# Two-layer cross-attention and expert kernel: hand-laced order of the first thirteen attention units, and a later rounding in steps 5, 9 and 13

## The reference

```python
ln_out = _ln(hidden_states, ln_w, ln_b)
q = _ln(_fp8_linear_pertensor(ln_out, wq, ...).reshape(b, s, g, hpg, d), qln_w, qln_b)
k = _ln(_fp8_linear_pertensor(ln_out, wk, ...).reshape(b, s, g, d), kln_w, kln_b)
v = _fp8_linear_pertensor(ln_out, wv, ...).reshape(b, s, g, d)
core = _gqa(q, k, v)            # self-attention, 16 query heads, 8 key heads
qx = _ln(_fp8_linear_pertensor(ln_out, wqx, ...))
kx, vx = split(cond @ w_kv_x)   # 64 context rows
xout = _gqa(qx, _ln(kx), vx)    # cross-attention, 16 query heads
catq = _div_clamp_fp8(concat([core, xout]), proj_smooth)
x = x + catq @ wproj * (proj_in_scale * proj_w_scale)
```

## Time and profile before

| | us |
|---|---|
| median of 3 runs | 832.49 (832.32 to 833.77) |
| the profiled execution | 832.6 |
| its span, first to last record | 830.8 |
| PE busy | 780.1 (94%) |
| DVE busy | 652.9 (79%) |
| ACT busy | 536.1 (65%) |
| POOL busy | 485.0 (58%) |

### The profile page before, as it was taken

One profiled execution on the slowest core, in us unless ns is written; L12 is line 12 of the kernel. 1 busy time (PEld: TensorE's weight loads), 2 busy tenths in 40 slices (PEclk: granted clock), 3 DMA queues, 4 the chain that ended last, 5 costly groups with the idle time before them and its releaser, 6 DMA issues.

```text
span 830.8 us, 14410 instructions
## 1 busy us (share of the span) xinstructions
PE 780.1 (94%) x4848; PEld 666.3 (80%) x4848; DVE 652.9 (79%) x1509; ACT 536.1 (65%) x1236; POOL 485.0 (58%) x858
## 2 busy tenths in 40 slices
PE   3588999999999999999999999999999999999997
PEld 2466788898788888888888878898888787777787
DVE  6878999899988999889889796676665658887644
ACT  6788887787877878778765465533332257986432
POOL 2588968859697696877876287425220124637510
PEclk9789999999999999999999999999999999999999
DMA  7000120011200112000200321986613000001001
GB/s 245 13 1 1 39 64 14 2 39 39 77 1 2 39 39 77 2 1 1 69 27 8 108 69 41 230 208 203 212 62 102 25 1 15 16 12 39 1 1 51
DMA packets 29224, 45.59 MB, mean 55 GB/s; under 512 B 4128, under 2 KB 18272, under 8 KB 29024
## 3 DMA queue, kind: packets, MB, share of 16 engines
q1 hardware_dynamic: 27760, 41.31, 16.8%
q10 hardware_dynamic: 1392, 3.37, 1.2%
HBM read 43.49 MB, written 1.18 MB: 54 GB/s over the span
## 4 chain that ended last, share of the span: by engine, by line
PE 64%; DVE 18%; ACT 9%; issue 4%; DMA 2%; SPq 1%; POOL 1%; ACTq 0%; DVEq 0%
PE PS L889 17%; PE PS L959 8%; PE PS L749 6%; PE PS L844 4%; PE PS L818 3%; PE PS L780 3%; PE PS L1073 3%; DVE st L1840 2%; PE PS L801 2%; PE PS L771 2%; PE PS L790 2%; PE PS L1025 2%; ACT P L1238 2%; DVE yb L1742 2%; PE PS L1035 1%
## 5 line engine op out<-in xcount | busy, mean ns | idle before, releaser
L2539 POOL TENSOR_SCALAR raw<-raw,mvq,rsq 128x128 f32<-128x128 f32 x312 | 183.7, 607 | 1.6
L889 PE MATMUL PS<-xq,WH 128*128 128x512 f32 x472 | 149.3, 398 | 0.0
L889 PEld LDWEIGHTS PS<-xq,WH 128*128 128x128 f32 x472 | 86.2, 189 | 17.5 <-issue 1.9
L749 PE MATMUL PS<-WH,xq 128*128 128x256 f32 (+1 forms) x256 | 88.5, 365 | 8.7 <-DVE xq L1746 6.2
L889 PE MATMUL PS<-xq,WL 128*128 128x512 f32 x236 | 92.7, 393 | 0.0
L749 PE MATMUL PS<-WL,xq 128*128 128x256 f32 (+1 forms) x256 | 84.7, 350 | 0.0
L1238 ACT ACTIVATE P<-PS,sm 128x256 f32<-128x256 f32 x128 | 61.1, 498 | 23.5 <-DVE sm L1904 23.4
L959 PE MATMUL PS<-xq,m_hh 128*128 128x256 f32 x384 | 70.2, 283 | 2.5 <-ACT m_hh L1124 1.3
L1840 DVE BATCH_NORM_STATS2 st<-raw 128x6 f32<-128x128 f32 x320 | 70.4, 276 | 1.7 <-ACT raw L1210 1.7
L818 PE MATMUL PS<-PT,vr 128*128 128x256 f32 x256 | 66.5, 382 | 3.8 <-ACT PT L1124 3.7
L780 PE MATMUL PS<-kT,qT 128*128 128x256 f32 x256 | 65.9, 380 | 1.9 <-ACT qT L1227 1.9
(11 more groups left out here) (316 smaller groups left out, 2154.7 us busy)
## 6 DMA issues: line engine op xcount, KB each, us to landing
wst<-in_wgu SPq DMA_DIRECT2D x24, 256.0 KB, 2.7
wst<-in_wall SPq DMA_DIRECT2D x18, 256.0 KB, 3.0
l_KM<-share SPq DMA_DIRECT2D x9, 384.0 KB, 3.7
dst<-in_wdn SPq DMA_DIRECT2D x24, 128.0 KB, 2.7
wst<-in_wkvx SPq DMA_DIRECT2D x8, 256.0 KB, 3.3
m_pre<-in_wo ACTq DMA_DIRECT2D x1, 2048.0 KB, 11.7
l_KM<-share SPq DMA_DIRECT2D x6, 256.0 KB, 6.6
l_S<-share SPq DMA_DIRECT2D x6, 256.0 KB, 6.2
```

What stands on the lines that cost most here:

```text
L749: t = e.matmul(PS[:, b, o:o + n], xq[s][:, k, c * 128:(c + 1) * 128], W[:, k, w0:w0 + n], start=(k == 0 and i == 0), stop=(k == 1 and i == 1))
L889: t = e.matmul(PS[:, b, :], W[wi][:, gu, k, :], a[:, k, cols], start=(n == 0), stop=(n == 5))
L2539: t = e.tensor_scalar(v, v, mvq[:, par, n, 0:1], rsq[:, par, n:n + 1], ALU.add, ALU.mult)
```

## The change

In all four lists the first thirteen units (n from 0 to 12, that is up to step 2, unit 2) are written out one call after another instead of coming from the loop, and the loops begin at BEGUN = 13. The calls are the same, in another order. On DVE the generators of quantise, stats, stats_x, begin_q, round_y and the layer norm are advanced one instruction at a time by go(generator, times); a, b and c are the stats of the three parts, q the quantisations, r the begin_q, y the roundings, lr the rest of the layer norm, xs stats_x. ln_root is rewritten so that its steps can be taken singly. On POOL norm_q is split into root_q (Newton) and norm_q(s, h) for one head, and the load_w of the next group's parts 4, 5 and 0 stand inside norm_q(2). DVE's semaphore for its own steps is no longer changed after the start. Apart from that, AHEAD loses (5, 4), (9, 4) and (13, 4): in these units DVE does the maxima first and then the rounding. The diff, cut:

```diff
@@ -18,6 +18,7 @@
 NEG = 1e30
 STEPS = 16
 PARTS = (2, 0, 1)
+BEGUN = 13
 P2ORDER = (4, 0, 1, 2, 3)
 QPAIRS = [(h, z) for h in range(4) for z in (1, 0)]
 SEG = [[(0, 0, 512, 0)], [(1, 512, 512, 0)], [(2, 1024, 256, 0), (3, 1280, 256, 256)]]
@@ -26,7 +27,7 @@
 NORMED_A = (0, 1, 2, 3)
 NPRE = 10
 WORDER = (4, 5, 0, 1, 2, 3)
-AHEAD = [(s, 4) for s in (2, 5, 6, 9, 10, 13)] + [(s, 2) for s in (3, 7, 11)]
+AHEAD = [(s, 4) for s in (2, 6, 10)] + [(s, 2) for s in (3, 7, 11)]
 ROUND = {5: (1, 4), 9: (1, 4), 13: (1, 4), 14: (1, 3), 15: (1, 3), 16: (1, 2)}
 
 
@@ -91,55 +92,123 @@
 
     do("ln", 0)
     do("kx", 0)
-    for q in range(3):
-        for c in range(2):
-            do("p1", 0, c, PARTS[q])
-        if q == 1:
-            do("ln", 1)
+    do("p1", 0, 0, 2)
+    do("p1", 0, 1, 2)
+    do("p1", 0, 0, 0)
+    do("p1", 0, 1, 0)
+    do("ln", 1)
+    do("p1", 0, 0, 1)
+    do("p1", 0, 1, 1)
...
+    do("ln", 3)
+    do("p2", 0, 4)
+    do("p2", 0, 0)
+    do("p1", 0, 4, 2)
+    do("p2", 0, 1)
+    do("p2", 0, 2)
+    do("p2", 0, 3)
+    do("scores", 0, 0)
+    do("p1", 0, 5, 2)
+    do("scores", 0, 1)
+    do("p1", 0, 4, 0)
+    do("scores", 0, 2)
+    do("p1", 0, 5, 0)
+    do("p1", 0, 4, 1)
+    do("p1", 0, 5, 1)
+    do("scores", 0, 3)
...
+    do("project", 0, 3)
+    do("p2", 3, 4)
+    do("values", 1, 4)
+    do("p1", 1, 0, 1)
+    do("turn", 2, 0)
+    do("p1", 1, 1, 1)
+    do("p2", 3, 0)
     units = [(s, k) for s in range(STEPS) for k in range(5)]
-    for n in range(len(units) + 5):
+    for n in range(BEGUN, len(units) + 5):
...
@@ -1328,54 +1397,131 @@
             load_w(0, 4)
+            load_w(0, 5)
             div(0)
-            load_w(0, 5)
             load_w(0, 0)
             div(1)
             load_w(0, 1)
             take_kx(0)
-            for c in range(2):
-                take_p1(0, c, PARTS[0])
+            take_p1(0, 0, 2)
+            load_p(0, 0)
+            load_p(0, 1)
+            take_p1(0, 1, 2)
...
+            div(5)
+            take_p1(0, 2, 0)
+            take_p1(0, 3, 0)
+            take_p1(0, 2, 1)
+            take_p1(0, 3, 1)
+            norm_a()
             take_vx(0)
+            take_p2(0, 4)
+            take_p2(0, 0)
+            div(6)
+            take_p2(0, 1)
+            take_p1(0, 4, 2)
+            exps(0, 0)
+            take_p1(0, 5, 2)
+            take_p1(0, 4, 0)
+            exps(0, 1)
+            take_p1(0, 5, 0)
+            take_p1(0, 4, 1)
+            take_p2(0, 2)
+            take_p1(0, 5, 1)
+            take_p2(0, 3)
+            exps(0, 2)
...
+            load_p(0, 3)
+            load_w(1, 4)
+            load_w(1, 5)
+            take_values(0, 2)
+            exps(0, 4)
+            take_turn(0, 3)
+            exps(1, 0)
...
@@ -1784,8 +1919,14 @@
 
             def ln_root(b2):
                 v, y, m = mv[:, b2, 1], rs[:, b2], nt[:, b2]
-                yield from ln_guess(b2, dv.sem)
-                yield from newton(v, y, m, dv.up())
+                guess = ln_guess(b2, dv.sem)
+                for _ in range(2):
+                    next(guess)
+                    yield
+                next(guess)
+                t = dv.up()
+                yield
+                yield from newton(v, y, m, t)
 
             def ln_guess(b2, signal):
                 v, y = mv[:, b2, 1], rs[:, b2]
@@ -1999,49 +2140,219 @@
-            weave(ln_rest_stats())
-            weave(quantise(0))
-            rest = ln_rest()
-            for c in range(6):
-                next(rest)
-            weave(quantise(1))
-            weave(rest)
-            weave(chain(*[lambda c=c, q=q: stats(0, c, PARTS[q]) for q in (0, 1) for c in (0, 1)]))
-            weave(stats_x(0))
-            weave(quantise(2))
-            weave(chain(*[lambda c=c: stats(0, c, PARTS[2]) for c in (0, 1)], lambda: begin_q(0)))
-            weave(quantise(3))
-            weave(quantise(4), chain(*[lambda c=c: stats(0, c, PARTS[0]) for c in (2, 3)]))
-            weave(chain(*[lambda c=c, q=q: stats(0, c, PARTS[q]) for q in (1, 2) for c in (2, 3)], lambda: begin_q(1)))
-
-            dv = Steps(sem("vector_attention"))
+            q = [quantise(n) for n in range(8)]
+            a, b, c = ([stats(n // 8, n % 8, j) for n in range(10)] for j in PARTS)
+            r = [begin_q(s) for s in range(5)]
+            y = [round_y(n // 2, n % 2) for n in range(6)]
+            ls, lr, xs = ln_rest_stats(), ln_rest(), stats_x(0)
+
+            def go(g, n=1):
+                for _ in range(n):
+                    next(g, None)
+
+            go(ls, 3)
+            go(q[0], 2)
...
+            go(lr, 5)
+            go(b[0])
+            go(lr, 2)
+            go(a[0])
+            go(xs)
+            go(a[0])
+            go(xs)
+            go(b[1], 2)
+            go(b[0])
+            go(a[1])
+            go(xs)
+            go(b[0])
+            go(b[1])
+            go(a[1])
+            go(q[2], 2)
+            go(b[1])
+            go(c[0])
+            go(q[2], 3)
+            go(c[0])
...
+            go(c[1])
+            go(b[0])
+            go(q[3])
+            go(r[0], 8)
+            go(q[4], 3)
+            go(b[2])
...
+            go(r[1], 8)
+            go(q[5], 2)
+            maxima(0, 0)
+            go(q[6])
+            load_p(0, 1)
+            maxima(0, 1)
+            go(a[4])
+            go(q[6], 2)
+            go(a[4])
+            go(a[5])
+            norm(0, 0)
+            norm(0, 1)
...
+            go(q[6])
+            go(b[5])
+            go(r[2], 8)
+            norm(0, 3)
+            go(q[7])
+            maxima(0, 4)
+            go(q[7], 3)
+            maxima(1, 0)
+            go(q[7])
+            norm(0, 4)
+            maxima(1, 1)
+            load_p(0, 2)
+            maxima(1, 2)
...
+            norm(2, 0)
+            go(b[8])
+            norm(2, 1)
+            add_o(0)
+            go(y[2])
+            go(b[8])
+            go(y[2])
+            go(b[8])
+            go(y[2])
+            go(a[8])
+            go(b[9])
+            go(y[2])
+            go(b[9], 2)
+            go(y[2])
+            go(a[8])
+            go(a[9])
+            go(b[9])
+
             units = [(s, k) for s in range(STEPS) for k in range(5)]
-            for n in range(len(units) + 5):
+            for n in range(BEGUN, len(units) + 5):
                 s, k = n // 5, n % 5
                 gp = s // 4
-                if 0 <= n - 1 < len(units):
+                if n - 1 < len(units):
                     norm(*units[n - 1])
                 z = int(k > ROUND.get(s, (2, 4))[0])
-                ahead = s > 1 and (s, k) in AHEAD
+                ahead = (s, k) in AHEAD
                 if ahead:
                     weave(round_y(s - 1, z))
                 if n < len(units):
                     maxima(s, k)
...
@@ -2522,7 +2833,7 @@
-            def norm_q(s):
+            def root_q(s):
...
+            def norm_q(s, h):
+                par = s % 2
+                for ci in range(2):
+                    v = raw[:, (2 * s + ci) % 4, h * 128:(h + 1) * 128]
+                    n = ci * 10 + h
+                    t = e.tensor_scalar(v, v, mvq[:, par, n, 0:1], rsq[:, par, n:n + 1], ALU.add, ALU.mult)
+                t.then_inc(scaled_q.sem, 1)
...
+            norm_q(2, 3)
+            norm_q(2, 4)
+            load_w(1, 4)
+            load_w(1, 5)
+            norm_q(2, 5)
+            load_w(1, 0)
+            norm_q(2, 6)
+            norm_q(2, 7)
+            root_q(3)
+            norm_q(3, 8)
...
                 for k in range(5):
+                    if 5 * s + k < BEGUN:
+                        continue
                     if s == 15 and k == 2:
...
                     if s + 2 < STEPS and k == 3:
-                        norm_q(s + 2)
+                        root_q(s + 2)
+                        for h in NORMED:
+                            norm_q(s + 2, h)
```

More of the change, by code:

```diff
@@ new lines, in attention_order @@
+    do("values", 0, 0)
+    do("turn", 0, 1)
+    do("p2", 1, 1)
+    do("kt", 0)
+    do("values", 0, 1)
+    do("turn", 0, 2)
+    do("p1", 0, 6, 2)
+    do("p2", 1, 2)
+    do("scores", 0, 4)
+    do("p1", 0, 7, 2)
+    do("values", 0, 2)
+    do("turn", 0, 3)
+    do("scores", 1, 0)
+    do("scores", 1, 1)
+    do("p2", 1, 3)
+    do("scores", 1, 2)
+    do("values", 0, 3)
+    do("p1", 0, 6, 0)
+    do("turn", 0, 4)
+    do("p1", 0, 7, 0)
+    do("p2", 2, 4)
+    do("scores", 1, 3)
+    do("p1", 0, 6, 1)
@@ new lines, in attention_order @@
+    do("values", 0, 4)
+    do("project", 0, 0)
+    do("turn", 1, 0)
+    do("p1", 0, 7, 1)
+    do("p2", 2, 0)
+    do("values", 1, 0)
+    do("turn", 1, 1)
+    do("scores", 1, 4)
+    do("p2", 2, 1)
+    do("project", 0, 1)
+    do("values", 1, 1)
+    do("scores", 2, 0)
+    do("turn", 1, 2)
+    do("p1", 1, 0, 2)
+    do("p2", 2, 2)
+    do("scores", 2, 1)
+    do("p1", 1, 1, 2)
+    do("values", 1, 2)
+    do("turn", 1, 3)
+    do("p2", 2, 3)
+    do("values", 1, 3)
+    do("p1", 1, 0, 0)
```

(54 more changed lines are left out.)

293 lines of the change are left out of this document (207 added, 86 removed).

## The result

| us | before | changed |
|---|---|---|
| median of the comparison | 832.4 (831.47 to 833.77) | 826.24 (825.18 to 829.93) |
| second comparison | 832.33 (830.38 to 835.75) | 826.3 (823.65 to 828.32) |
| profiled execution / its span | 832.6 / 830.8 | 829.93 / 828.1 |
| `values(2,0)`, end of the prefix on PE | 116.93 | 113.04 |

The ratio is 0.9935 [0.9906, 0.9963], in the second comparison 0.9919 [0.99, 0.9939]: faster by 6 us (0.7%), clear of the spread, where 7.2 us and 825.3 were forecast. The profiled execution was the longest of its comparison, 3.7 us above the median. So I read the mechanisms in it, and their sizes in it and in a second profile of the same kernel (`after_again`, span 825.7).

The account below looks back on a forecast made before the run. The opening was taken as bound by a loop through all engines, DVE fullest, and the rest by PE. Gains of 5.0 and 2.2 us sum to 7.2, taking 832.6 to 825.4, or 825.3 against the median; range 820.8 to 830.2.

Parts of the forecast that it names:

- Part one: Opening, first thirteen units: reordered lists on all four engines gain 5.0 us, bounds 0 and 8.2.
- I put it 2 us later than its 51.70: Opening on PE: scores(0,0) starts 2 us later, since begin_q(0) follows the fourth quantisation and POOL starts norm_q(0) later.
- DVE is the fullest member: Opening, 28 to 120.7 us: DVE is busy 79.2 of 92.7 us, so its queue sets the 5.0 us gain.
- POOL's 2.93: Opening: POOL's one long wait, 2.93 us for begin_q(2), was to be gone.
- Part two: Steps 5, 9 and 13: rounding behind the maxima gains 2.2 us, from -0.3 to 3.3.
- What it gains before it keeps, as long as DVE follows: After the opening: PE keeps what it gained, as DVE has 2.2 us to spare in a full step.
- 0.6 net: Step 13: the swap gains 0.6 us net, as PE's 1.30 us wait before values(13,4) shrinks by 0.7 to 0.9.
- A: Opening: waits only change their place, part one gives 1 us, total 829.3; chance 0.13.
- B: Everything closes: PE's 8.2 us plus part two's 2.2 to 3.3, total 821.5; chance 0.16.
- C: Part two gives nothing, as project(4,2) loses what values(5,3) gains, total 827.5; chance 0.09.
- D: norm_q(1) to norm_q(3): DVE and POOL collisions make it slower, 835.0; sign: over 14 us for twenty scalings; chance 0.06.
- E: Whole kernel: the order is in effect the same for PE, no change, 832.5; chance 0.04.

Follow-up runs that it names:

- rounding_only: The kernel before with only the rounding put behind the maxima in steps 5, 9 and 13; 831.13 us, ratio 0.9993.
- begin_q_early: The changed kernel with begin_q(0) ahead of the last instruction of the fourth quantisation on DVE; 826.07 us.
- opening_only: The changed kernel with the rounding ahead of the maxima again in steps 5, 9 and 13; 826.59 us, ratio 0.9925.
- ahead_all_off: The changed kernel with the rounding behind the maxima in steps 6 and 10 too; 826.25 us.
- keep_13: The changed kernel with the rounding of step 13 ahead of the maxima again; 826.06 us.

## Why the prediction held, and which steps of it did not

**Part one, 5.0 us.** The size held, its working did not. At values(2,0) the new list is ahead by 116.93 - 112.10 = 4.8 us, or 3.7 against rounding_only. Of this 2.1 (0.9) lie before p1(0,2,0): begin_q(0) now follows the fourth quantisation, and PE waits 1.7 us for that instead of 4.1 (3.1 in begin_q_early, which puts begin_q(0) back before its last instruction). The prediction counted only the price of this move, POOL's later start. From p1(0,2,0) to values(2,0) it is 75.42 before and 72.66 in after_again: 2.8.
- "I put it 2 us later than its 51.70": it was 3.5 to 3.8 in the two profiles of the changed kernel (and 2.5 to 3.3 in opening_only, ahead_all_off and keep_13, which have its opening). The waits that make it are 3.8 for POOL and 1.2 for ACT, with 1.0 more at p2(0,1) in the first profile, against 0.27 and 1.85 before; the rest is 2.6 us of PE work brought ahead of the scores. The step that failed left out that banks 2, 5 and 6 are shared: take_vx delays p2 through the bank, not only take_p2 by its place in the queue.
- "DVE is the fullest member": not behind the scores. From there to values(2,0) PE idles 2.5 to 2.7 us in all twelve profiles with the new opening, nearly all of it for ACT, and DVE idles more, 3.4 to 5.5. Nine of the twelve take 56.6 to 57.0 us, whatever was done ahead of it; the other three (57.4 to 58.0) are those in which the lower clock reaches 1.7 to 3.0 us into it. So the gain is that PE idles 5.8 us less there and has 2.6 us of its work in front, less the late start, and not DVE's share; the 1.4 us taken off for the waits stood near the right sum by luck. Which of the opening's many moves closed which wait was not tried singly.
- Of the pause expected "about as long as the 1.75 us", 1.10 stayed before the third quantisation, with 1.20 before the statistics ahead of it.
- POOL's 2.93 fell to 1.15, not to 0. DVE begins norm(2,2) 4.7 us earlier in the first profile (115.92 instead of 120.61).

**Part two, 2.2 us.** The mechanism of step 5 was right: the 1.25 and the 0.79 are gone, and a new wait of 0.70 stands at project(4,2), forecast at 0.9. Two terms failed. "What it gains before it keeps, as long as DVE follows" was said of the prefix and silently used for step 5: 0.9 of the 1.5 us went again at turn(6,4) and behind, where DVE's slower instructions made it late. That wait is the one named as a sign that DVE did not follow. And "0.6 net" for step 13 was -0.5: I took DVE's free time from step 5, where it runs late; in step 13 it runs early, and the maxima wait for PE with the rounding behind them. In rounding_only steps 5 and 9 gave 1.2 us each instead of 0.8, so that with -0.5 the part comes to 1.9: near 2.2, but by errors that cancel. On top of the new opening it is 0.6 to 2.4 us by the profile taken. The medians do not show the part: 826.59 without it, 826.3 with it.

**The total.** 4.8 + 0.6 = 5.4 by the stages of after_again; the medians say 6. The 0.9 us by which the forecast missed is within what the medians can tell.

**The rivals.** A (waits only move, 829.3) describes the late start but not what came behind. B (all closes, 821.5) fails: of its 8.2 us 2.5 stayed, and in front of them, from 28 to 52.8, PE idled 8.4 us where 7.3 were. C (part two gives nothing, 827.5): its mechanism is contradicted in step 5, where 1.5 us were won, but that the part is worth next to nothing in the end the medians cannot exclude. D needed slower scalings: those of norm_q(3) did take 14.13 us for twenty, over the 14 that I had named as its sign, but those of norm_q(2) 9.10 + 1.04 + 1.83 = 12.0 (13.26 before), and PE did not wait for either. E was not the case. DVE's instructions are slower beside POOL's in places: the multiplication of norm(6,4) took 0.96 us for 0.71, and the small instruction before it 0.34 for 0.17. The Trainium skill, page "SBUF — State Buffer", section "Who interferes with whom", has the two engines exclude each other for whole instructions where both use the ports that they share; the trace agrees, down to the small instructions that end 23 ns behind POOL's scalings, but in begin_q_early the same instructions run through a scaling unhindered, and where they were held it cost PE 0.5 us at turn(6,4), not the 8.0 us that D needed.
